# An attention-and-feed-forward kernel on one core: output spectra to POOL and in halves to DVE, second-norm rounding to ACT, the choice of delays in one pass

## The reference, cut to what matters

```
xn   = layernorm(x)
q, k, v = xn Wq' + bq, ctx Wk' + bk, ctx Wv' + bv
corr = irfft(rfft(q) * conj(rfft(k))).mean over the 16 values of a head   # [batch, head, 512 delays]
w, delays = top_k(corr, 6);  w = softmax(w)
out[t] = sum_i w[i] * v[(t - delays[i]) mod 512]                           # circular, per head
x1   = x + out Wo' + bo
z    = layernorm(x1)
h    = gelu(bitlinear(z, W1, b1))        # 256 -> 1024
y    = x1 + bitlinear(h, W2, b2)         # 1024 -> 256
bitlinear(a, W, b): a is RMS-normed and rounded to 8-bit steps of its row's greatest value (127/max),
                    W to -1, 0, 1 times its mean absolute value; then matmul and bias
```

## Time and profile before

| | |
|---|---|
| median of 3 runs | 181.0 us (180.97 to 183.41) |
| the profiled execution | 182.84 us, its span 180.8 us |
| PE busy / PEld | 159.7 / 107.1 us |
| DVE busy | 149.8 us |
| ACT busy | 89.7 us |
| POOL busy | 83.9 us |
| chain that ended last, shares | PE 25%, DVE 24%, issue 7%, POOL 1% |

### The profile page before, as it was taken

One profiled execution on the slowest core, in us unless ns is written; L12 is line 12 of the kernel. 1 busy time (PEld: TensorE's weight loads), 2 busy tenths in 40 slices (PEclk: granted clock), 3 DMA queues, 4 the chain that ended last, 5 costly groups with the idle time before them and its releaser, 6 DMA issues.

```text
span 180.8 us, 2886 instructions
## 1 busy us (share of the span) xinstructions
PE 159.7 (88%) x869; PEld 107.1 (59%) x877; DVE 149.8 (83%) x347; ACT 89.7 (50%) x158; POOL 83.9 (46%) x150
## 2 busy tenths in 40 slices
PE   7989889998999998999994977993799999999943
PEld 2635667657655956576873755670456766555632
DVE  1537299999299996999979999779997999999992
ACT  3136615548722441211510521519449999999821
POOL 6030899754440003932009827071985654454430
PEclk9999999999999999999999999999589999999999
DMA  5999989080474000000000001616447101111012
GB/s 191 319 289 391 359 289 190 3 116 0 64 107 61 5 0 0 0 0 5 2 0 0 0 0 29 91 29 87 64 59 115 58 29 58 44 45 62 29 58 87
DMA packets 14128, 15.07 MB, mean 83 GB/s; under 512 B 1186, under 2 KB 13347, under 8 KB 14116
## 3 DMA queue, kind: packets, MB, share of 16 engines
q1 hardware_dynamic: 9892, 10.73, 17.9%
q0 software_dynamic: 4224, 4.19, 15.8%
HBM read 8.61 MB, written 2.10 MB: 59 GB/s over the span
## 4 chain that ended last, share of the span: by engine, by line
PE 25%; DVE 24%; issue 7%; POOL 1%; DVEq 1%; ACT 0%; POOLq 0%
PE psum L469 4%; PE psum L458 4%; DVE c_f L1046 4%; PE psum L518 4%; PE psum L538 3%; DVE res L1061 2%; DVE hmax L1035 2%; DVE stats L910 2%; PE psum L520 2%; PE psum L338 2%; PE psum L529 2%; DVE prod_sum L763 1%; DVE xmax L924 1%; DVE m_b L884 1%; DVE out_f L891 1%
## 5 line engine op out<-in xcount | busy, mean ns | idle before, releaser
L390 PE MATMUL psum<-wkv,c_f 128*128 128x512 f32 x64 | 29.0, 598 | 0.8 <-ACT c_f L580 0.8
L1035 DVE TENSOR_REDUCE hmax<-wf 128x1 f32<-128x1025 f32 x16 | 19.4, 1211 | 0.7 <-ACT wf L683 0.7
L390 PEld LDWEIGHTS psum<-wkv,c_f 128*128 128x128 f32 x64 | 11.8, 190 | 13.7 <-issue 12.4
L683 ACT ACTIVATE wf<-psum,xdeq 128x1024 f32<-128x1024 f32 x16 | 17.6, 1101 | 1.3 <-PE psum L520 1.3
L599 ACT COPY kv_f<-psum 128x512 f32<-128x512 f32 x16 | 9.1, 582 | 18.4 <-PE psum L390 18.4
L691 ACT ACTIVATE x_f<-wf 128x1024 f32<-128x1024 f32 x16 | 16.9, 1056 | 0.0
L458 PE MATMUL psum<-to_signal,out_f 128*128 128x256 f32 x64 | 14.6, 382 | 2.4 <-POOL out_f L1170 2.4
L518 PE MATMUL psum<-w1q,xq_t 128*128 128x512 bf16 x59 | 16.2, 392 | 0.5 <-issue 0.3
L538 PE MATMUL psum<-w2q,kv_f 128*128 128x256 bf16 x128 | 16.4, 273 | 0.0
L469 PE MATMUL psum<-wo,out_t 128*128 128x256 f32 x64 | 14.9, 386 | 1.3 <-DVE out_t L898 1.3
L403 PE MATMUL psum<-wq,x_f 128*128 128x256 f32 x64 | 15.1, 381 | 0.8 <-ACT x_f L580 0.8
(11 more groups left out here) (164 smaller groups left out, 351.0 us busy)
## 6 DMA issues: line engine op xcount, KB each, us to landing
ctx_in<-in_ctx SPq DMA_DIRECT2D x4, 512.0 KB, 5.1
res<-in_x SPq DMA_DIRECT2D x4, 512.0 KB, 6.5
res<-bo_all POOLq DMA_DIRECT2D x4, 512.0 KB, 5.2
res<-b_all POOLq DMA_DIRECT2D x4, 512.0 KB, 5.9
out<-res SPq DMA_DIRECT2D x16, 128.0 KB, 1.7
wf<-in_w_t SPq DMA_DIRECT2D x1, 1024.0 KB, 8.3
wf<-in_w_t SPq DMA_DIRECT2D x2, 512.0 KB, 9.7
wkv<-in_wkv_t SPq DMA_DIRECT2D x1, 512.0 KB, 7.5
```

Source lines behind the costliest of these rows:

```text
L390: mm = pe.matmul(bank(K_BANKS + ft), c_f[:, c, ft * P:(ft + 1) * P], wkv[:, c, :], start=(c == 0), stop=(c == NC - 1))
L683: act.activation(hid[j], hb, ACT.Gelu, scale=xdeq[:, m, j:j + 1]).then_inc(s["hid_made"], 1)
L1035: dve.tensor_reduce(hmax[:, j:j + 1], hid_and_least[j], AX.X, ALU.max, apply_absolute_value=True).then_inc(s["hmax_made"], 1)
```

## The change

- The output spectra of batches 0, 1 and 3 are made whole on POOL (`out_spectrum`, six operations each), real and imaginary part.
- That of batch 2, the leading one of the late group (`FIRST_LATE`), is made whole on DVE, first for the columns of c = 0, then for c = 1 (`out_spectrum_halves`, twelve operations of 256 elements), and `inverse(2, c)` waits for its own half only.
- `out_f` has two buffers, by the parity of the batch.
- The rounding of the second norm (`xround`) moves from DVE to ACT (`round_x`), with a scale of -127 / max made by one more small DVE operation (`x_scales`). The cast to bf16 stays on DVE (`whole_x`), now behind `x_deq`.
- The choice of delays: chosen values are replaced by a sentinel below all others (`TAKEN`), and one operation compares with it, multiplies with the exponentials and sums. L835 goes, L841's place is taken by a `scalar_tensor_tensor`. Instead of scaling the [32, 512] weights (L846), a [32, 32] diagonal of reciprocals is made, and `turn_g` multiplies by it instead of transposing with the identity.

```diff
             def turn_g(g):
...
-                    mm = pe.transpose(psum[:, G_BANKS[g], a * GR:(a + 1) * GR], chosen[:, a * P:(a + 1) * P], eye[0:GR, 0:GR])
+                    mm = pe.matmul(psum[:, G_BANKS[g], a * GR:(a + 1) * GR], chosen[:, a * P:(a + 1) * P], g_diag[:],
+                                   start=True, stop=True)
...
             def inverse(n, c):
-                if c == 0:
-                    pe.wait_ge(s["out_re_made"], n + 1)
-                    pe.wait_ge(s["out_im_made"], n + 1)
+                if n == FIRST_LATE:
+                    pe.wait_ge(s["out_half_made"], 2 * c + 2)
+                elif c == 0:
+                    pe.wait_ge(s["out_re_made"], by_pool(n))
+                    pe.wait_ge(s["out_im_made"], by_pool(n))
...
+            def round_x(n):
+                act.wait_ge(s["xscale_made"], n + 1)
+                if n:
+                    act.wait_ge(s["xq_made"], n)
+                for a in range(NA):
+                    ins = act.activation(xround[:, a, :], xc[:, n % 2, a, :], ACT.Identity, scale=xscale[:, a:a + 1])
+                ins.then_inc(s["xround"], 1)
...
             centre(1)
+            round_x(0)
             copy_x(0)
             inverse_copy(3, 0)
             inverse_copy(3, 1)
+            round_x(1)
             centre(2)
             copy_x(1)
...
                     if t == 0:
+                        round_x(2)
                         centre(3)
                     if t == 1:
                         copy_x(2)
+                        round_x(3)
...
-                dve.match_replace(rest[:], top[:], corr[:], -1.0e38).then_inc(s["rest_made"], 1)
+                dve.match_replace(rest[:], top[:], corr[:], TAKEN).then_inc(s["rest_made"], 1)
...
-                dve.tensor_tensor(rest[:, 0:L], corr[:, 0:L], rest[:, 0:L], ALU.not_equal).then_inc(s["mask_made"], 1)
...
-                dve.tensor_tensor_reduce(out=expd[:], in0=expd[:], in1=rest[:, 0:L], scale=1.0, scalar=0.0,
-                                         op0=ALU.mult, op1=ALU.add, accum_out=gsum[:]).then_inc(s["gsum_made"], 1)
+                dve.scalar_tensor_tensor(chosen[:], rest[:, 0:L], TAKEN, expd[:], ALU.is_le, ALU.mult,
+                                         accum_out=gsum[:]).then_inc(s["gsum_made"], 1)
...
-                dve.tensor_scalar(chosen[:], expd[:], grec[:, 0:1], None, ALU.mult).then_inc(s["g_made"], 1)
+                dve.tensor_scalar(g_diag[:], eye[0:GR, 0:GR], grec[:, 0:1], None, ALU.mult).then_inc(s["g_made"], 1)
...
+            def out_spectrum_halves(n):
+                dve.wait_ge(s["g_ready"], n // (NB // NG) * 3 + 3)
+                dve.wait_ge(s["at_done"], n * 4 - 6)
...
+                for c in range(NC):
+                    h = slice(c * H // NC, (c + 1) * H // NC)
+                    cols = slice(c * P, (c + 1) * P)
+                    dve.tensor_tensor(m[0][:, :, h], v[0][:, :, h], g_r[:, :, h], ALU.mult)
+                    dve.tensor_tensor(m[1][:, :, h], v[1][:, :, h], g_i[:, :, h], ALU.mult).then_inc(s["m_half_made"], 1)
+                    dve.tensor_tensor(m[2][:, :, h], v[1][:, :, h], g_x[:, :, h], ALU.mult)
+                    dve.tensor_tensor(m[3][:, :, h], v[0][:, :, h], g_i[:, :, h], ALU.mult).then_inc(s["m_half_made"], 1)
+                    dve.wait_ge(s["m_half_made"], 2 * c + 1)
+                    dve.tensor_tensor(out_f[:, n % 2, :, 0, cols], m_halves[:, 0, :, cols], m_halves[:, 1, :, cols],
+                                      ALU.subtract).then_inc(s["out_half_made"], 1)
+                    dve.wait_ge(s["m_half_made"], 2 * c + 2)
+                    dve.tensor_tensor(out_f[:, n % 2, :, 1, cols], m_halves[:, 2, :, cols], m_halves[:, 3, :, cols],
+                                      ALU.add).then_inc(s["out_half_made"], 1)
...
             combine_g(0)
             copy_g_spectrum(0)
-            out_re_products(0)
-            out_re(0)
             multiply(3)
             cross_spectra(1)
             inverse_out(0, 0)
             inverse_out(0, 1)
-            out_re_products(1)
-            out_re(1)
             choose(1)
...
-            out_re_products(2)
-            out_re(2)
+            out_spectrum_halves(FIRST_LATE)
             stats2(0)
             mean_var2(0)
             for n in (2, 3):
...
                 row_max(n - 2)
+                x_scales(n - 2)
                 inverse_out(n, 0)
-                x_inverse(n - 2)
                 inverse_out(n, 1)
-                if n + 1 < NB:
-                    out_re_products(n + 1)
-                    out_re(n + 1)
-                quantise_x(n - 2)
                 x_deq(n - 2)
+                whole_x(n - 2)
...
+            def out_spectrum(n):
+                if n != 1:
                     pool.wait_ge(s["g_ready"], n // (NB // NG) * 3 + 3)
                 if n:
+                    pool.wait_ge(s["out_re_made"], by_pool(n) - 1)
+                    pool.wait_ge(s["out_im_made"], by_pool(n) - 1)
+                pool.tensor_tensor(by_heads(m_a[:]), v_of(n, 0), g_of(g_re, n), ALU.mult)
+                pool.tensor_tensor(by_heads(m_b[:]), v_of(n, 1), g_of(g_im, n), ALU.mult).then_inc(s["m_ab"], 1)
                 pool.tensor_tensor(by_heads(m_c[:]), v_of(n, 1), g_of(g_rx, n), ALU.mult)
                 pool.tensor_tensor(by_heads(m_d[:]), v_of(n, 0), g_of(g_im, n), ALU.mult).then_inc(s["m_cd"], 1)
+                if n > 1:
+                    pool.wait_ge(s["at_done"], n * 4 - 6)
+                pool.wait_ge(s["m_ab"], by_pool(n))
+                pool.tensor_tensor(out_f[:, n % 2, :, 0, :], m_a[:], m_b[:], ALU.subtract).then_inc(s["out_re_made"], 1)
+                pool.wait_ge(s["m_cd"], by_pool(n))
+                pool.tensor_tensor(out_f[:, n % 2, :, 1, :], m_c[:], m_d[:], ALU.add).then_inc(s["out_im_made"], 1)
...
-            for n in (0, 1):
-                out_im_products(n)
-                out_im(n)
-            out_im_products(2)
-            out_im(2)
+            out_spectrum(0)
+            out_spectrum(1)
+            out_spectrum(3)
             x_rms(0)
-            out_im_products(3)
-            out_im(3)
             aug_parts(0)
```

More of the change, by code:

```diff
@@ L46 @@
 NPART = 6
+FIRST_LATE = NB // NG
 B_SEG = 16
@@ L49 @@
 ABSENT = -3.0e38
+TAKEN = -3.4e38
 X_LEAST = EPS * EPS
@@ L457, in inverse @@
                     fam, part = divmod(ft, 2)
-                    mm = pe.matmul(psum[:, I_BANKS + c, fam * D:(fam + 1) * D], out_f[:, fam, part, c * P:(c + 1) * P],
+                    mm = pe.matmul(psum[:, I_BANKS + c, fam * D:(fam + 1) * D], out_f[:, n % 2, fam, part, c * P:(c + 1) * P],
                                    to_signal[:, ft, :], start=(ft == 0), stop=(ft == 3))
@@ L869, in copy_g_spectrum @@
                 dve.memset(g_im[0:1, 0, r], 0.0).then_inc(s["g_ready"], 1)
[L871 to L883, removed]
-                dve.tensor_tensor(by_heads(m_b[:]), v_of(n, 1), g_of(g_im, n), ALU.mult).then_inc(s["m_ab"], 1)
@@ L886, in out_re @@
-            def out_re(n):
-                dve.wait_ge(s["m_ab"], n + 1)
-                if n:
-                    dve.wait_ge(s["at_done"], n * 4 - 2)
-                dve.tensor_tensor(out_f[:, :, 0, :], m_a[:], m_b[:], ALU.subtract).then_inc(s["out_re_made"], 1)
+            def out_spectrum_halves(n):
+                dve.wait_ge(s["g_ready"], n // (NB // NG) * 3 + 3)
+                dve.wait_ge(s["at_done"], n * 4 - 6)
+                v = [by_heads(kv_f[:, n, part:part + 3:2, D:2 * D]) for part in range(2)]
+                g_r, g_i, g_x = [g[:, :, bass.ds(n * H, H)].unsqueeze(3).broadcast_to([P, 2, H, DK]) for g in (g_re, g_im, g_rx)]
+                m = [by_heads(m_halves[:, k]) for k in range(4)]
+                for c in range(NC):
[11 more added lines that the diff above has]
+                                      ALU.add).then_inc(s["out_half_made"], 1)
@@ L924, in row_max, with x_scales @@
                 dve.tensor_reduce(xmax[:], xc_and_least[:, n % 2, :, 0:D + 1], AX.X, ALU.max, apply_absolute_value=True).then_inc(s["xmax_made"], 1)
-            def x_inverse(n):
+            def x_scales(n):
                 dve.wait_ge(s["xmax_made"], n + 1)
                 dve.reciprocal(xinv[:], xmax[:]).then_inc(s["xinv_made"], 1)
+                dve.wait_ge(s["xinv_made"], n + 1)
+                if n:
+                    dve.wait_ge(s["xround"], n)
+                dve.tensor_scalar(xscale[:], xinv[:], -127.0, None, ALU.mult).then_inc(s["xscale_made"], 1)
             def x_deq(n):
@@ L937, in x_deq, with whole_x @@
                 dve.reciprocal(s_full[:], xdeq[:, n]).then_inc(s["s_full_made"], 1)
-            def quantise_x(n):
-                dve.wait_ge(s["xinv_made"], n + 1)
-                if n:
-                    dve.wait_ge(s["xq_made"], n)
-                for a in range(NA):
-                    ins = dve.tensor_scalar(xround[:, a, :], xc[:, n % 2, a, :], xinv[:, a:a + 1], -127.0, ALU.mult, ALU.mult)
-                ins.then_inc(s["xround"], 1)
```

(9 more changed lines are left out.)

26 lines of the change are left out of this document (11 added, 15 removed).

## The result

The changed kernel takes 190.9 us (median of 4 runs, 189.05 to 191.98), the kernel before 181.45 in the same comparison (180.97 to 183.41). The ratio is 1.047, with a 95% interval of 1.034 to 1.059: slower. It compares the means of the fast runs and leaves out the one slow run of the changed kernel, the 191.98, so it is less than the ratio of the medians. The profiled execution of the changed kernel took 189.05 us, with a span of 187.1; the one of before took 182.84, with a span of 180.8.

A forecast was written before the change was run, and what follows sets the result against it. PE's list was taken to bound the kernel from 77.5 to 94 us, then DVE and POOL. Terms 2.5 + 6.0 + 1.3 = 9.8 us, added to the 181.0 median, gave 190.8 us; range 183.5 to 193.5.

The forecast's parts named there:

- strict turns between DVE and POOL: DVE operations on two SBUF inputs and POOL operations never run at once; each waits for the whole of the other's.
- T: The end of the third g_ready of group 1 (L869), 94.5 us in the kernel before.
- Before T: Up to the third g_ready of group 1: late inverse(0), slowed cross operations, turn_g(1) as matmuls; 2.5 us later, bounds 1.6 to 3.1.
- After T: From the third g_ready of group 1 to the maximum of tile 3: DVE's halves alternate with POOL; 6.0 us later.
- The lost wait for aug: Before turn_x(0): PE's wait of 1.22 us for POOL's aug goes, as aug is ready before project(2) ends.
- The rule of the Trainium skill on the turns: An exclusive lock between a DVE instruction with two SBUF inputs and a GpSimd instruction that reads SBUF.
- The clock: PE idle before inverse(2) and project(2) may drop to 1.2 GHz; 1.3 us lost, bounds 0 and 2.6.
- The first fall: PE's clock falls in 4.8 us idle before inverse(2); hidden, since even at half speed it ends at T + 14.6.
- DVE not held back: Rival: DVE's 256-element halves go first or turns are uneven, so no slower, 182.5 us; chance 0.11.
- The lock in part: Rival: DVE gets two short operations in each of POOL's gaps, 2.5 us less, no clock fall, 187 us; chance 0.17.
- The clock low into inverse(3): Rival: as forecast, but PE's clock also stays low into inverse(3), 193 to 195 us; chance 0.08.
- DVE's released time as a gain: Rival: about 8 us released on DVE shortens the path by over 2%, 177 us; chance 0.04.

The follow-up runs named there:

- apart with fillers: Changed kernel with POOL's spectra of batches 1 and 3 made to wait for DVE, and twelve more fillers between inverse(2) and project(2): 184.3 us, ratio 1.012.
- rounding alone: Kernel before with only the second norm's rounding moved to ACT, with x_scales and whole_x: 181.1 us, ratio 0.989.
- all four roundings: Kernel before with rounding on ACT for all four batches and batch 3's spectrum whole on POOL: 181.1 us, ratio 0.996.
- two roundings: Kernel before with rounding on ACT for batches 0 and 1 only, two out_f buffers and batch 3's spectrum whole on POOL: 181.6 us, ratio 0.994.
- both spectra apart: Changed kernel, but POOL starts batch 1's spectrum after the cross spectra and batch 3's after DVE's batch 2: 184.5 us, ratio 1.013.

## Why the prediction was right, step by step

The forecast was 190.8 us. Its mechanism, strict turns between DVE and POOL, held in both places where they meet. That the number came within 0.1 us of the median is luck: the sizes below show errors that cancel.

**What bounded the kernel.** The two profiled executions differ before the change touches anything: the last part of q(3), the same code in both, starts at 75.81 us before and at 74.64 after, 1.17 us ahead. The row is in the timeline of PE of the kernel before:

```profile
24.98 0.49 PE L328 MATMUL psum<-forward,c_even 128*128 128x128 f32 x2 [0.77 <-POOL c_even L1117]
```

In the changed kernel the same group starts at 23.85 with no idle time. The forecast took the profiled execution of before as one like the others; the comparisons of T below add the 1.17 us.

**Before T: 2.5 forecast, 2.87 measured** (1.70 in the traces, plus 1.17). inverse(0) came 1.00 us late (forecast 1.1). correlate(1) added 1.16, the 1.77 less the 0.61 of the earlier trace rows (forecast 0.95): three of the four cross operations had their turn to wait, not four (the first took 0.30 us). From inverse(0) to turn_g(1) that makes 1.24 with what surrounds it, and from turn_g(1) to T 0.63 (forecast 0.45), nearly all of it the turn itself: 1.07 less 0.43 is 0.64. The forecast took four distances of 0.22 for it and left out the length of the last matmul. The rule of the Trainium skill (TensorE: Matmul & The Clock Gate, Terms) that was weighed there, transposes four times faster, would by an estimate have given 1.3; the trace shows a factor of 2.5, so the measurement decides for the rows.

**After T: 6.0 forecast, 4.88 measured.** The term that was mis-sized is the time for which a POOL product holds DVE. I took 1.0 us, its spacing when it runs alone; a pair of turns takes 1.20, and with 0.34 of DVE that leaves 0.86. That is 0.8 of the 1.1 us; the other 0.3 lie behind turn_x(0), where the forecast lost 0.1 and the trace gained 0.2. So the first half was ready at T + 6.65 (forecast 7.3), all at T + 9.7 (10.5), project(2) began at T + 17.4 (18.1), turn_x(0) at T + 20.9 (21.8), and the maximum of tile 3 at T + 48.2 (49.3); before it was T + 43.3. The lost wait for aug came as forecast. The rule of the Trainium skill on the turns (SBUF — State Buffer, Who interferes with whom), as the prediction gives it, for a DVE instruction with two SBUF inputs, agrees with every row of the halves. The waiting copies before T have one.

**The clock: 1.3 forecast, 0 measured in the profiled execution.** The first fall came and was hidden. The second did not come there, but it did in the profiles of six variants at this place: project(2) took 6.03, 5.41 (three times), 5.34 and 5.26 us instead of 3.72. So its price is 1.5 to 2.3 us, a little under the bound of 2.6, and that it comes in some profiles and not in others is what the term of 1.3, half of its bound, stood for. How often it comes in unprofiled runs of the changed kernel is not shown.

**The sum.** By the traces 2.87 + 4.88, less 0.28 in the rest of the feed-forward part, is 7.5 us, against 9.8 forecast. The medians differ by 9.5, and by the ratio the difference is 8.5 (interval 6.2 to 10.7). The profiled execution of after was the fastest of its four runs, 1.9 us under their median, and that of before 1.4 over its median. The collision at 25 us is worth 1.1 of such differences; the clock before project(2) would fill most of the rest, but that is argued, not shown.

**The rivals.** DVE not held back (182.5) fell: the halves took 1.28 us beside POOL. The lock in part (187) fell: one DVE operation in each gap of POOL, never two. The clock low into inverse(3) was not seen. DVE's released time as a gain (177) fell: its busy time is 5.6 us less and the time is longer. The one part that gained alone, the rounding, gave 1.0 us in the traces, mostly by a wait of PE that the spectra take away as well, so even that gain is not seen in the whole.

## What to carry to other kernels

Before a step of elementwise work is moved to GpSimd, look at what VectorE does at that moment with operands in SBUF. Where they met a GpSimd instruction, those with two such operands, one of four elements included, and some with one, a copy of 32 elements and a scaling of four, waited for its end; MAX8 and MATCH_REPLACE8 did not. So look at their lengths in a trace, and take as the price the number of those that meet one times GpSimd's operation; a finer cut of VectorE's work meets more of them. Either order the two so that they do not meet, or move work to ScalarE: it took the rounding, and though DVE's cast then waits up to 1.36 us for it, 1.0 us was gained when that was the only change. Test the parts of a change apart: here one of three lost nearly all, and one that gained about 1 us alone took away a wait that another part took away too, so that gains did not add.

## What the runs showed of the hardware

A POOL product of 512 elements holds DVE for 0.86 us, though products alone follow each other at 1.02: some 0.16 us of each overlaps with the other engine's turn.

The length of an idle time does not alone decide whether the clock falls. It fell at the end of idle times of 2.31 and 2.42 us (apart with fillers, rounding alone) and 0.2 us behind one of 2.39 (all four roundings). It stayed up through 2.39 (two roundings), 2.42 (kernel before) and 3.17 (kernel after), and it fell at project(1) of the kernel with both spectra apart with no idle time over 0.16 us in the 3.3 us before. What else decides was not found. Fillers held the clock through inverse(2) and did not hold it before project(2).

An execution can lose 1.1 us to a chance meeting of POOL and DVE at 25 us: PE waits 0.64 to 1.01 us for c_even there in six of the fourteen profiles, though the code there is the same in all; the other eight show no wait there and start that group between 23.85 and 24.41. In the kernel before the first x_even took DVE 0.94 us there and the first c_even took POOL 1.22; in the changed kernel they took 0.41 and 0.72. A difference of one profiled execution each should be read from an anchor behind that place.
